# Decoder block on one core: x's rows at a pitch of 532 floats, a plain half-size message addition, and x's second layout loaded in one burst

## The chip, the core and the metric

The kernel runs on one core of one Trainium2 chip. The metric is the device time of one execution in microseconds (us). The kernel before took 665.99 us, the median of three runs (665.76 to 666.15). One more execution was recorded by the hardware profiler; every row shown here is from that one.

## What is computed

x has 32 batches of 64 channels by 512 positions, all float32. The reference is a decoder block of three layers, each added to its input and normalised over the 512 positions:

```python
q = jnp.transpose(x, (2, 0, 1))                       # 512 x 32 x 64
scores = jnp.einsum('lnc,lmc->lnm', q, q) / sqrt(64)  # for each position l: 32 x 32
prob = softmax(scores, axis=-1)
msg = jnp.einsum('lnm,lmc->lnc', prob, q)
x = _layernorm(x + (x + msg^T))                       # first layer, "x1"
x = _layernorm(x + xattn(x, ctx, Wq, Wk, Wv, Wo, bo, g))
x = _layernorm(x + ffn(x, w_gate, w_up, w_down))      # weights and activations quantised by groups of 32
```

The change is in the first layer. There the attention runs over the 32 batches, once for each of the 512 positions, so every operand of its small matrix products takes one float of each batch's row.

## The kernel before, in words

The five engines have their programs written out by hand, in a fixed order, and wait for each other on semaphores. SP (SyncE) issues all the transfers. The names and lines that matter:

- **x in SBUF.** `xt` holds x with two batches side by side on 128 partitions (64 channels each) and 16 rows of 512 floats along the partition, so from one batch's row to the next it is 2048 bytes. `xsw` behind it is the same with the two halves swapped; `both_x` and `x_by_batch` are views over both (L124 to L130). `load_x` (L375) brings x in four pieces; ScalarE (`swap_up`) and VectorE (`swap_down`, L1123) copy each piece across.
- **x's second layout.** `xq` (L131) has the batches on partitions: `load_xq` (L378) is called 32 times, 128 KB each. With three semaphores taken in turn, SP waits before transfer n until transfer n-3 has landed. Behind these on SP's queue stand `load_aw(1)`, `load_aw(2)`, `load_item(2)`, `load_aw(3)` and the first two context loads (L452 to L457).
- **The first layer.** The 512 positions go in 8 chunks of 16 positions from each quarter. `scores(c)` (TensorE, L2837) makes 64 products, each with a 64x32 stationary and a 64x32 moving operand read from `both_x` and `x_by_batch` with one float per 2048-byte row. `shift_scores` (VectorE, L1133 and L1134) takes the row maximum off, `exp_scores` (ScalarE, L1986) the exponential, `sum_scores` (VectorE, L1139 and L1140) the reciprocal sum, `norm_scores` (GpSimd, L631) scales, `transpose_probs` (VectorE, L1146) turns 32x32 blocks, and `spread_probs` (ScalarE, L1980) writes four masked copies with the mask `quarter` as scale. `messages(c, h)` (TensorE, L2865) multiplies them with `xq`, and `add_msg(c, h)` (VectorE, L1154) forms 2x + msg in `xt`. `scores(c)` from c = 2 on waits for `shift_scores(c-2)`.
- **TensorE's order**: scores(0), two weight transposes (L2792), scores(1) to scores(4), `project_wo` (L2798), scores(5), `project_b` (L2807), scores(6), scores(7), and then the messages, with transposes of the quantised weights and the first logits of the second layer between them. `messages(0, 0)` waits for all of `xq` (L2855).
- **VectorE's order** around it: shift(0), `scale_aw(0)` (a grouped maximum over 128x1376, L1087), `scale_item(0)`, sum(0), shift(1), clip_item(0), transpose(0), shift(2), sum(1), clip_aw(0), sum(2), transpose(1), shift(3), shift(4), sum(3), transpose(2), shift(5), and so on: the weights are quantised between the steps of the softmax.
- **The norm.** `x1_stats` and `x1_rsqrt` (L634) take mean and variance of a row and add `eps_tile` (1e-5).
- From about 112 us on the second layer (16 tiles of 128 rows) and then the FFN follow, with the same kind of hand-written order.

Of the kernel before, what the change touches and what calls it, by code (L numbers as in the profile page):

```python
# [8 lines left out]
ALU = mybir.AluOpType  # L9
# [9 lines left out]
P = 128  # L19
# [18 lines left out]
def decoder_kernel(nc, x, ctx_in, Wq, Wk, Wv, Wo, bo, g, w_gate, w_up, w_down, out):  # L38
    B, C, L = x.shape
    HID, DIM = Wq.shape  # L40
# [4 lines left out]
    T = B * C // P  # L45
    NJ = HID // P
    NT = L // P
# [9 lines left out]
    LG = L // 4  # L57
    CL = 16
    CQ = 8
    CHUNKS = LG // CL  # L60

    with ExitStack() as stack:
        def sb(name, shape, dt=F32):
            return stack.enter_context(nc.sbuf_tensor(name, shape, dt))

        def sem(name):
            return stack.enter_context(nc.semaphore(name))

        banks = stack.enter_context(nc.psum_tensor("banks", [P, 8, 512], F32))
        bank = [banks[:, i] for i in range(8)]  # L70
# [17 lines left out]
        shift = sb("shift", [P, 1])  # L88
        neg_mean = sb("neg_mean", [P, 1])
# [4 lines left out]
        square_o = sb("square_o", [P, 2])  # L94
        mv = sb("mv", [P, 2])
        eps_tile = sb("eps_tile", [P, 1])
        quarter = sb("quarter", [P, 4])
        vare = sb("vare", [P, 1])
        rstd = sb("rstd", [P, 1])
# [3 lines left out]
        mv1 = sb("mv1", [P, 2])  # L103
        vare1 = sb("vare1", [P, 1])
        rstd1 = sb("rstd1", [P, 1])
        mv2 = sb("mv2", [P, 2])
        vare2 = sb("vare2", [P, 1])
        rstd2 = sb("rstd2", [P, 1])
        neg_mean1 = sb("neg_mean1", [P, 1])
        shift1 = sb("shift1", [P, 1])  # L110
        neg_mean2 = sb("neg_mean2", [P, 1])
        shift2 = sb("shift2", [P, 1])

        AREA = 42400
        big = sb("big", [P, AREA])
        off = 0

        def cut(n):
            nonlocal off
            off += n  # L120
            assert off <= AREA
            return big[:, off - n:off]

        both_x = big[:, 0:2 * T * L].rearrange("p (n l) -> p n l", n=B)  # L124
        x_pairs = big[:, 0:2 * T * L].rearrange("p (s t l) -> p t s l", s=2, t=T)
        x_by_batch = (x_pairs[0:C], x_pairs[C:P, :, ::-1])

        xt = cut(T * L).rearrange("p (t l) -> p t l", t=T)

        xsw = cut(T * L).rearrange("p (t l) -> p t l", t=T)  # L130
        xq = cut(C * LG).rearrange("p (c l) -> p c l", c=C)  # L131

        off = T * L
        EK = cut(4 * NJ * L).rearrange("p (s b j n) -> p s b j n", s=2, b=2, j=NJ)
        EQ = cut(4 * NT * HID).rearrange("p (s b i h) -> p s b i h", s=2, b=2, i=NT)
        et_at = off
# [38 lines left out]
        off = sc_at  # L175
        sc = cut(3 * CL * B).rearrange("p (k l m) -> p k l m", k=3, l=CL)
        assert off <= sc_end
        off = et_at
        pT = cut(3 * CL * B).rearrange("p (k l m) -> p k l m", k=3, l=CL)
        assert off <= et_end  # L180
        off = pd_at
        pd = cut(2 * CL * P).rearrange("p (k l j m) -> p k l j m", k=2, l=CL, j=4)
        assert off <= aw_at
        off = aw_at
# [9 lines left out]
        won = wg_area[0:C, NJ * 7 * C:NJ * 7 * C + HID]  # L194
        woT = wg_area[:, NJ * 7 * C + HID:NJ * 8 * C + HID].rearrange("p (t c) -> p t c", t=NJ)

        off = T * L
        hs = cut(4 * FFN).rearrange("p (s n) -> p s n", s=4)
        h8 = cut(FFN // 4).bitcast(FP8)
        hk = [[cut(GH) for _ in range(3)] for _ in range(2)]  # L200
        spare = cut(L)
        assert off <= T * L + 4 * NJ * L

        off = T * L + 4 * NJ * L
        hq = cut(FT * P).bitcast(BF16).rearrange("p (s n) -> p s n", s=2)
        hqT = cut(FT * P).bitcast(BF16).rearrange("p (s f t) -> p s f t", s=2, f=FT)
        xo = cut(2 * L).rearrange("p (s n) -> p s n", s=2)
        assert off <= T * L + 4 * NJ * L + 2 * NT * HID
        yo = cut(2 * L).rearrange("p (s n) -> p s n", s=2)
        assert off <= T * L + 4 * (NJ * L + NT * HID)  # L210

        s = Semaphores()

# [17 lines left out]
        s.g8_ready = sem("g8_ready")  # L231

        s.x_loaded = [sem(f"x_loaded_{piece}") for piece in range(4)]
        s.xq_loaded = [sem(f"xq_loaded_{turn}") for turn in range(3)]
        s.swapped_up = sem("swapped_up")
        s.swapped_down = sem("swapped_down")
        s.scores_ready = sem("scores_ready")
# [135 lines left out]
        def _(sp):  # L373
# [3 lines left out]

            def load_xq(n):  # L378
                c, j = CQ * (n // 4), n % 4
                if n >= 3:  # L380
                    sp.wait_ge(s.xq_loaded[n % 3], 16 * (n // 3))
                sp.dma_start(xq[B * j:B * j + B, c:c + CQ], x[:, c:c + CQ, LG * j:LG * j + LG]).then_inc(s.xq_loaded[n % 3], 16)

            def load_aw(a):
                if a >= 3:
# [64 lines left out]
            for n in range(4 * C // CQ):  # L450
                load_xq(n)
# [120 lines left out]
        def _(pool):  # L572
            ch = Chain(pool, s.pool_chain)
            ch.link(pool.memset(ident[:], 0.0))
            ch.link(pool.affine_select(out=ident[:], in_=ident[:], compare_op=ALU.not_equal, fill=1.0, base=0,
                                       pattern=[[-1, P]], channel_multiplier=1))
            pool.tensor_copy(ident_bf[:], ident[:]).then_inc(s.consts, 1)
            pool.memset(eps_tile[:], 1e-5).then_inc(s.consts, 1)
            ch.link(pool.memset(quarter[:], 0.0))
            for j in range(4):  # L580
                ch.link(pool.memset(quarter[B * j:B * j + B, j:j + 1], 1.0))
            pool.memset(minus_half[:], -0.5).then_inc(s.consts, 1)
            ch.link(pool.memset(pair_ones[:], 0.0))
            for h in range(2):
# [46 lines left out]
                pool.tensor_tensor(p, p, s_sum[:, c % 3].unsqueeze(2).to_broadcast([P, CL, B]), ALU.mult  # L631
                                   ).then_inc(s.probs_ready, 1)

            def rsqrt(t, var, read, mv, vare, neg_mean, rstd, shift, done):  # L634

                pool.wait_ge(var, t + 1)
                if t:
                    pool.wait_ge(read, t)
                pool.tensor_tensor(neg_mean[:], zero[:], mv[:, 0:1], ALU.subtract)
                ch.link(pool.tensor_tensor(vare[:], mv[:, 1:2], eps_tile[:], ALU.add))  # L640
                ch.link(pool.tensor_tensor(rstd[:], vare[:], minus_half[:, 0:1], ALU.pow))
                pool.tensor_tensor(shift[:], neg_mean[:], rstd[:], ALU.mult).then_inc(done, 1)

            def x1_rsqrt(t):
                rsqrt(t, s.x1_var, s.x1_ready, mv1, vare1, neg_mean1, rstd1, shift1, s.x1_rstd)

            def x2_rsqrt(t):
                rsqrt(t, s.x2_var, s.x2_ready, mv2, vare2, neg_mean2, rstd2, shift2, s.x2_rstd)

            def fold_p(f, i):  # L650
                pool.wait_ge(s.q_exp_done, 4 * f + i + 1)
# [79 lines left out]
            shift_aw(4)  # L731
            shift_aw(5)
            x1_rsqrt(0)
            x1_rsqrt(1)
            dequant_aw(4)
            shift_aw(6)
            x1_rsqrt(2)
            fold_p(0, 0)
            dequant_aw(5)
# [343 lines left out]
        def _(dve):  # L1083
            ch = Chain(dve, s.dve_chain)
# [63 lines left out]

            def add_msg(c, h):
                dve.wait_ge(s.msg_ready, 2 * c + h + 1)  # L1150
                m = bank[(2, 6)[c % 2] + h].rearrange("p (l q) -> p q l", l=CL // 2)
                l0 = CL * c + CL // 2 * h
                r = xt.rearrange("p t (j l) -> p (t j) l", j=4)[:, :, l0:l0 + CL // 2]
                dve.scalar_tensor_tensor(out=r, in0=r, scalar=2.0, in1=m, op0=ALU.mult, op1=ALU.add  # L1154
                                         ).then_inc(s.msg_added, 1)

            def ln_stats(src, st, mv, done):
# [1626 lines left out]
        def _(pe):  # L2785
# [65 lines left out]
            def messages(c, h):  # L2851
                if h == 0:
                    pe.wait_ge(s.pd_ready, c + 1)
                if c == 0 and h == 0:
                    for turn in range(3):  # L2855
                        pe.wait_ge(s.xq_loaded[turn], 16 * len(range(turn, 4 * C // CQ, 3)))
                if c == 1 and h == 0:
                    pe.wait_ge(s.b_copied, 2)
                if c >= 2:
                    pe.wait_ge(s.msg_added, 2 * c + h - 3)  # L2860
                o = bank[(2, 6)[c % 2] + h]
                for l in range(CL // 2):
# [837 lines left out]
```

## Time and profile before

| | us |
|---|---|
| median of 3 runs | 665.99 |
| the profiled execution | 667.34 |
| its span in the trace | 665.5 |
| TensorE busy | 608.4 (91%) |
| VectorE busy | 559.1 (84%) |
| ScalarE busy | 486.0 (73%) |
| GpSimd busy | 481.9 (72%) |

The span is what the trace covers; the rest of the profiled time lies around it. TensorE is named PE in the rows, VectorE DVE, ScalarE ACT, GpSimd POOL. PEclk is TensorE's granted clock as a share of 2.4 GHz. A TensorE product of float32 operands appears as two records in the trace, so 64 products are 128 records.

### The profile page before, as it was taken

What the parts mean: (1) busy time and instruction counts of PE and PEld (TensorE: products, weight loads), DVE (VectorE), ACT (ScalarE), POOL (GpSimd) and SP (SyncE); (2) the same over time, 40 slices, a digit from 0 to 9 for tenths busy, and PEclk for the clock granted to TensorE, in tenths of its full rate; (3) what the DMA queues carried; (4) which work ended last, traced back from release to release, by engine and by line L of the source; (5) the groups of instructions that cost most, each with busy time, mean ns of one, the idle gap of its engine ahead of it and who ended that gap; (6) DMA issues with size and microseconds to landing.
All of it is one profiled execution on the core that took longest, in us unless ns stands there. A gap on an engine that the chain in (4) does not pass through costs nothing. (4 is left out here: it accounts for less than half of the span.)

```text
span 665.5 us, 13176 instructions
## 1 busy us (share of the span) xinstructions
PE 608.4 (91%) x4864; PEld 334.4 (50%) x4864; DVE 559.1 (84%) x801; ACT 486.0 (73%) x871; POOL 481.9 (72%) x634
## 2 busy tenths in 40 slices
PE   0757999889999999999999999999999979999993
PEld 0756997344444544455544455445444634444441
DVE  2779898799999999998998878888788369999992
ACT  5459664788899989888988879888888725443535
POOL 1165957679889989998888596786678544776673
PEclk9957999899999999999999999999999989999998
DMA  9547131000010011110101000000000003445645
GB/s 296 159 136 225 44 88 56 0 17 25 1 42 31 10 33 40 41 49 22 35 12 45 1 23 17 7 17 17 0 1 1 9 8 63 80 87 101 133 105 131
DMA packets 62912, 36.77 MB, mean 55 GB/s; under 512 B 45184, under 2 KB 53376, under 8 KB 62848
## 3 DMA queue, kind: packets, MB, share of 16 engines
q1 hardware_dynamic: 62848, 35.93, 21.5%
q8 instruction: 39, 0.64, 0.4%
q14 instruction: 25, 0.20, 0.1%
HBM read 21.82 MB, written 4.19 MB: 39 GB/s over the span
## 5 line engine op out<-in xcount | busy, mean ns | idle before, releaser
L1932 ACT ACTIVATE big<-banks 128x512 f32<-128x512 f32 x288 | 158.6, 601 | 22.0 <-PE banks L2923 8.9
L663 POOL TENSOR_TENSOR big<-big 128x512 f32<-128x512 f32 x128 | 132.3, 1061 | 21.2 <-DVE big L1187 21.0
L1164 DVE TENSOR_REDUCE big<-banks 128x1 f32<-128x512 f32 x128 | 83.1, 680 | 25.0 <-PE banks L2880 24.8
L1993 ACT ACTIVATE big<-banks,big 128x512 f32<-128x512 f32 x128 | 88.0, 695 | 19.3 <-DVE big L1164 18.1
L655 POOL TENSOR_TENSOR big<-big 128x512 f32<-128x512 f32 x64 | 82.2, 1289 | 10.1 <-ACT big L1998 10.0
L1170 DVE TENSOR_REDUCE big<-banks 128x16 f32<-128x1024 f32 x64 | 77.1, 1205 | 4.4 <-PE banks L2890 4.4
L1175 DVE TENSOR_TENSOR big<-banks,big 128x1024 f32<-128x1024 f32 x64 | 78.3, 1223 | 2.7 <-PE banks L2923 0.7
L2913 PEld LDWEIGHTS banks<-ident,big 128*128 128x128 f32 x512 | 56.6, 142 | 46.8 <-issue 22.3
L2923 PEld LDWEIGHTS banks<-ident,big 128*128 128x128 f32 x512 | 55.3, 141 | 46.6 <-issue 22.7
L2913 PE MATMUL banks<-ident,big 128*128 128x128 f32 x512 | 74.2, 281 | 2.6 <-ACT big L1993 1.5
L1998 ACT ACTIVATE big<-big 128x1024 f32<-128x1024 f32 x64 | 68.2, 1065 | 10.2 <-DVE big L1175 9.7
L2923 PE MATMUL banks<-ident,big 128*128 128x128 f32 x512 | 73.8, 280 | 1.5 <-ACT big L1932 1.2
L2880 PE MATMUL banks<-big,WkT 64*128 64x512 f32 x256 | 72.6, 644 | 0.1
L2890 PE MATMUL banks<-WqT,big 64*128 64x512 f32 x256 | 68.3, 610 | 3.4 <-ACT big L2027 2.4
L590 POOL TENSOR_SCALAR big<-big 128x16 f32<-128x16 f32 (+3 forms) x55 | 22.7, 412 | 63.4 <-DVE big L1088 38.0
L2937 PE MATMUL banks<-big 128*64 128x512 f32 x256 | 64.0, 606 | 0.4 <-issue 0.4
L2960 PE MATMUL banks<-big 128*64 128x512 f32 x256 | 60.6, 602 | 1.3 <-DVE big L1195 1.3
L2073 ACT ACTIVATE big<-banks 128x448 f32<-128x448 f32 (+1 forms) x48 | 26.1, 548 | 45.7 <-PE banks L2986 45.7
L2847 PE MATMUL banks<-big 64*32 64x32 f32 x1024 | 31.1, 314 | 27.8 <-ACT big L1932 16.5
L1092 DVE TENSOR_SCALAR big<-big 128x512 fp8e4<-128x512 f32 (+3 forms) x55 | 43.1, 785 | 12.3 <-POOL big L618 5.3
L2986 PE MATMUL banks<-wg_area,big 128*128 128x448 bf16 (+1 forms) x192 | 45.9, 362 | 4.3 <-DVE big L1235 4.3
L2986 PE MATMUL banks<-wuT,big 128*128 128x448 bf16 (+1 forms) x192 | 46.0, 363 | 0.0
(108 smaller groups left out, 1126.0 us busy)
## 6 DMA issues: line engine op xcount, KB each, us to landing
big<-in_x_dram SPq DMA_DIRECT2D x4, 1024.0 KB, 8.8
big<-in_x_dram SPq DMA_DIRECT2D x32, 128.0 KB, 2.8
big<-in_ctx_dram SPq DMA_DIRECT2D x16, 256.0 KB, 2.7
out_dram<-big SPq DMA_DIRECT2D x16, 256.0 KB, 2.4
big<-in_L_ffn_w_down_dram SPq DMA_DIRECT2D x4, 688.0 KB, 5.8
big<-in_L_ffn_w_gate_dram SPq DMA_DIRECT2D x10, 256.0 KB, 2.8
big<-in_L_ffn_w_up_dram SPq DMA_DIRECT2D x10, 256.0 KB, 3.0
big<-big SPq DMA_TRANSPOSE x48, 2.7
```

What stands on the lines that cost most here:

```text
L655: pool.tensor_tensor(qfold[:, i % 2], e[:, :, :, 0:DH // 2], e[:, :, :, DH // 2:DH], ALU.add).then_inc(s.q_folded, 1)
L663: pool.tensor_tensor(e, e, r, ALU.mult).then_inc(s.p_ready, 1)
L1164: dve.tensor_reduce(kneg[:, par, i:i + 1], bank[par], X, ALU.max, negate=True).then_inc(s.k_max_ready, 1)
L1170: ch.link(dve.tensor_reduce(qmax[:, i], q_pair, X, ALU.max))
L1175: dve.tensor_tensor(EQ[:, f % 2, :, i].rearrange("p b (h d) -> p b h d", d=DH), q_pair, qmax[:, i].unsqueeze(3).to_broadcast([P, 2, HEADS, ...
L1932: return act.activation(dst, src, ACT.Copy)
L1993: act.activation(EK[:, f % 2, par, i], bank[par], ACT.Exp, bias=kneg[:, par, i:i + 1], accum_out=ksum[:, f % 2, par, i:i + 1]).then_inc(s. ...
L2880: pe.matmul(bank[par][:], WkT[rows, P * i:P * i + P], ctxs[rows, f % 2], start=True, stop=True).then_inc(s.klog_ready, 1)
L2890: pe.matmul(bank[2 + par][:], xt[rows, f, P * i:P * i + P], WqT[rows, :], start=True, stop=True).then_inc(s.qlog_ready, 1)
L2913: last = pe.transpose(bank[4 + n % 2][:, P * j:P * j + P], EK[:, t % 2, par, j, P * i:P * i + P], ident[:])
L2923: last = pe.transpose(bank[4 + n % 2][:, P * i:P * i + P], EQ[:, t % 2, par, i, P * j:P * j + P], ident[:])
L2986: last = pe.matmul(o[:, 0:w], xqT[:, u % 2, f], wT[:, f, c0:c0 + w], start=(f == 0), stop=(f == KT - 1))
```

## The change

The rows of `xt` and `xsw` are laid 532 floats (2128 bytes) apart instead of 512; all areas behind them move up by 320 floats, and `pT`, which lay at the end of `xq` and at the start of `ET` at once, is anchored to the end of `xq`. The 32 transfers of `xq` all count on one semaphore and SP no longer waits between them; TensorE waits for that one. The mask holds 0.5 instead of 1.0, so the message comes out at half size, and the addition is x + msg/2 without the factor 2; as its result is half of 2x + msg, the norm adds a quarter of the epsilon, from a new one-column tile.

```diff
+        LP = L + 20
+        AREA = 42400 + T * (LP - L)
-        both_x = big[:, 0:2 * T * L].rearrange("p (n l) -> p n l", n=B)
-        x_pairs = big[:, 0:2 * T * L].rearrange("p (s t l) -> p t s l", s=2, t=T)
+        both_x = big[:, 0:2 * T * LP].rearrange("p (n l) -> p n l", n=B)
+        x_pairs = big[:, 0:2 * T * LP].rearrange("p (s t l) -> p t s l", s=2, t=T)
-        xt = cut(T * L).rearrange("p (t l) -> p t l", t=T)
-        xsw = cut(T * L).rearrange("p (t l) -> p t l", t=T)
+        xt = cut(T * LP).rearrange("p (t l) -> p t l", t=T)[:, :, 0:L]
+        xsw = cut(T * LP).rearrange("p (t l) -> p t l", t=T)[:, :, 0:L]
+        xq_end = off
-        off = et_at
+        off = xq_end
         pT = cut(3 * CL * B).rearrange("p (k l m) -> p k l m", k=3, l=CL)
...
-        s.xq_loaded = [sem(f"xq_loaded_{turn}") for turn in range(3)]
+        s.xq_loaded = sem("xq_loaded")
             def load_xq(n):
                 c, j = CQ * (n // 4), n % 4
-                if n >= 3:
-                    sp.wait_ge(s.xq_loaded[n % 3], 16 * (n // 3))
-                sp.dma_start(xq[B * j:B * j + B, c:c + CQ], ...).then_inc(s.xq_loaded[n % 3], 16)
+                sp.dma_start(xq[B * j:B * j + B, c:c + CQ], ...).then_inc(s.xq_loaded, 16)
...
+            pool.memset(eps_half[:], 0.25e-5)
-                ch.link(pool.memset(quarter[B * j:B * j + B, j:j + 1], 1.0))
+                ch.link(pool.memset(quarter[B * j:B * j + B, j:j + 1], 0.5))
-                ch.link(pool.tensor_tensor(vare[:], mv[:, 1:2], eps_tile[:], ALU.add))
+                ch.link(pool.tensor_tensor(vare[:], mv[:, 1:2], eps[:], ALU.add))
...
             def add_msg(c, h):
                 dve.wait_ge(s.msg_ready, 2 * c + h + 1)
-                m = bank[(2, 6)[c % 2] + h].rearrange("p (l q) -> p q l", l=CL // 2)
+                m = bank[(2, 6)[c % 2] + h].rearrange("p (l t j) -> p t j l", l=CL // 2, t=T)
                 l0 = CL * c + CL // 2 * h
-                r = xt.rearrange("p t (j l) -> p (t j) l", j=4)[:, :, l0:l0 + CL // 2]
-                dve.scalar_tensor_tensor(out=r, in0=r, scalar=2.0, in1=m, op0=ALU.mult, op1=ALU.add
-                                         ).then_inc(s.msg_added, 1)
+                r = xt.rearrange("p t (j l) -> p t j l", j=4)[:, :, :, l0:l0 + CL // 2]
+                dve.tensor_tensor(r, r, m, ALU.add).then_inc(s.msg_added, 1)
...
-                    for turn in range(3):
-                        pe.wait_ge(s.xq_loaded[turn], 16 * len(range(turn, 4 * C // CQ, 3)))
+                    pe.wait_ge(s.xq_loaded, 16 * 4 * C // CQ)
```

## Rows read from the trace of the kernel before

**Rows 1.** The page: TensorE's busy share, and the chain that ended last, by engine.

```profile
PE 608.4 (91%) x4864; PEld 334.4 (50%) x4864; DVE 559.1 (84%) x801; ACT 486.0 (73%) x871; POOL 481.9 (72%) x634
PE 7%; POOL 3%; DVE 2%; issue 1%; DMA 1%; ACT 1%; SPq 0%; POOLq 0%; DVEq 0%; ACTq 0%
```

**Rows 2.** Busy time by stretch: length, each engine's busy time, PEclk, DMA share, GB/s.

```profile
16.50:66.40 49.90, 34.79 (x1068) 33.45 (x1068) 40.04 (x36) 32.85 (x19) 21.60 (x14) 0.72 0.60 174
66.40:111.60 45.20, 45.20 (x553) 41.27 (x550) 40.26 (x59) 27.06 (x46) 33.84 (x32) 0.97 0.23 58
...
140.00:550.00 410.00, 400.85 (x2616) 201.12 (x2617) 355.86 (x524) 343.83 (x665) 330.15 (x423) 1.00 0.08 21
```

**Rows 3.** TensorE's timeline, 16 to 68 us: start, length, engine, line, operation, idle before.

```profile
16.51 3.95 PE L2847 MATMUL banks<-big 64*32 64x32 f32 x128 [16.51 <-ACT big L1932]
20.39 1.64 PE L2792 MATMUL banks<-ident,wg_area 128*128 128x128 f32 x8
21.95 7.55 PE L2847 MATMUL banks<-big 64*32 64x32 f32 x256
33.26 3.93 PE L2847 MATMUL banks<-big 64*32 64x32 f32 x128 [3.76 <-DVE big L1134]
...
55.66 1.61 PE L2807 MATMUL banks<-wg_area 64*64 64x64 f32 x32 [3.27 <-ACT wg_area L1932]
...
63.95 2.53 PE L2847 MATMUL banks<-big 64*32 64x32 f32 x78 [1.40 <-issue]
```

**Rows 4.** VectorE's timeline, 20 to 80 us.

```profile
21.83 8.18 DVE L1087 TENSOR_REDUCE big<-big 128x43 f32<-128x1376 f32 x1
...
32.52 0.69 DVE L1134 TENSOR_TENSOR big<-banks,big 128x512 f32<-128x512 f32 x1
...
49.10 3.42 DVE L1134 TENSOR_TENSOR big<-banks,big 128x512 f32<-128x512 f32 x1
...
52.55 0.69 DVE L1139 TENSOR_REDUCE big<-big 128x16 f32<-128x512 f32 x1
...
57.05 4.67 DVE L1146 STREAM_TRANSPOSE big<-big 128x512 f32<-128x512 f32 x1
60.13 3.33 DVE L1087 TENSOR_REDUCE big<-big 128x43 f32<-128x1376 f32 x1
...
66.59 0.72 DVE L1146 STREAM_TRANSPOSE big<-big 128x512 f32<-128x512 f32 x1
67.24 1.55 DVE L1087 TENSOR_REDUCE big<-big 128x43 f32<-128x1376 f32 x1
```

**Rows 5.** ScalarE's exponential: its first call, and one beside the messages.

```profile
21.95 7.30 ACT L1986 ACTIVATE big<-big 128x512 f32<-128x512 f32 x1 [5.49 <-DVE big L1134]
...
74.55 0.65 ACT L1986 ACTIVATE big<-big 128x512 f32<-128x512 f32 x1
```

**Rows 6.** Busy time by stretch, inside scores(1) and over scores(3); columns as in rows 2.

```profile
21.95:25.70 3.75, 3.75 (x134) 3.75 (x137) 3.75 (x1) 3.75 (x2) 0.00 (x0) 1.00 0.66 152
...
33.26:37.20 3.94, 3.93 (x128) 3.78 (x128) 0.00 (x0) 3.84 (x1) 3.69 (x4) 0.50 0.59 169
```

**Rows 7.** TensorE's timeline: three half chunks of messages.

```profile
74.32 7.49 PE L2865 MATMUL banks<-big 128*64 128x64 f32 x96
```

**Rows 8.** SP's timeline: the 32 transfers of xq, and the first one behind them.

```profile
19.04 34.76 SPq L382 DMA_DIRECT2D big<-in_x_dram  x32
53.84 0.93 SPq L388 DMA_DIRECT2D big<-in_L_ffn_w_down_dram  x2
```

**Rows 9.** Transfers while SP waits in turn, 24 to 54 us: queue's bytes and share, issues.

```profile
q1 hardware_dynamic: 7766, 3.74, 45.2%
...
big<-in_x_dram SPq DMA_DIRECT2D x29, 128.0 KB, 2.8
```

**Rows 10.** Busy time by stretch where the transfer engines are full; columns as in rows 2.

```profile
57.00:61.00 4.00, 4.00 (x142) 3.88 (x142) 4.00 (x3) 3.68 (x3) 3.79 (x1) 0.50 0.98 394
```

**Rows 11.** VectorE's message addition: calls, shortest, median and longest duration in ns.

```profile
L1154 DVE SCALAR_TENSOR_TENSOR big<-big,banks x16: 627/680/689, 72.4 to 110.7; 128x512 f32<-128x512 f32 x16
```

More of the change, by code:

```diff
@@ L96, in decoder_kernel @@
         eps_tile = sb("eps_tile", [P, 1])
+        eps_half = sb("eps_half", [P, 1])
         quarter = sb("quarter", [P, 4])
@@ L112, in decoder_kernel @@
         shift2 = sb("shift2", [P, 1])
-        AREA = 42400
+        LP = L + 20
+        AREA = 42400 + T * (LP - L)
         big = sb("big", [P, AREA])
@@ L122, in cut @@
             return big[:, off - n:off]
-        both_x = big[:, 0:2 * T * L].rearrange("p (n l) -> p n l", n=B)
-        x_pairs = big[:, 0:2 * T * L].rearrange("p (s t l) -> p t s l", s=2, t=T)
+        both_x = big[:, 0:2 * T * LP].rearrange("p (n l) -> p n l", n=B)
+        x_pairs = big[:, 0:2 * T * LP].rearrange("p (s t l) -> p t s l", s=2, t=T)
         x_by_batch = (x_pairs[0:C], x_pairs[C:P, :, ::-1])
-        xt = cut(T * L).rearrange("p (t l) -> p t l", t=T)
-        xsw = cut(T * L).rearrange("p (t l) -> p t l", t=T)
+        xt = cut(T * LP).rearrange("p (t l) -> p t l", t=T)[:, :, 0:L]
+        xsw = cut(T * LP).rearrange("p (t l) -> p t l", t=T)[:, :, 0:L]
         xq = cut(C * LG).rearrange("p (c l) -> p c l", c=C)
-        off = T * L
+        xq_end = off
+        off = T * LP
         EK = cut(4 * NJ * L).rearrange("p (s b j n) -> p s b j n", s=2, b=2, j=NJ)
@@ L195, in decoder_kernel @@
         woT = wg_area[:, NJ * 7 * C + HID:NJ * 8 * C + HID].rearrange("p (t c) -> p t c", t=NJ)
-        off = T * L
+        off = T * LP
         hs = cut(4 * FFN).rearrange("p (s n) -> p s n", s=4)
@@ L201, in decoder_kernel @@
         spare = cut(L)
-        assert off <= T * L + 4 * NJ * L
-        off = T * L + 4 * NJ * L
+        assert off <= T * LP + 4 * NJ * L
+        off = T * LP + 4 * NJ * L
         hq = cut(FT * P).bitcast(BF16).rearrange("p (s n) -> p s n", s=2)
@@ L207, in decoder_kernel @@
         xo = cut(2 * L).rearrange("p (s n) -> p s n", s=2)
-        assert off <= T * L + 4 * NJ * L + 2 * NT * HID
+        assert off <= T * LP + 4 * NJ * L + 2 * NT * HID
         yo = cut(2 * L).rearrange("p (s n) -> p s n", s=2)
-        assert off <= T * L + 4 * (NJ * L + NT * HID)
+        assert off <= T * LP + 4 * (NJ * L + NT * HID)
         s = Semaphores()
@@ L379, in load_xq @@
                 c, j = CQ * (n // 4), n % 4
-                if n >= 3:
-                    sp.wait_ge(s.xq_loaded[n % 3], 16 * (n // 3))
-                sp.dma_start(xq[B * j:B * j + B, c:c + CQ], x[:, c:c + CQ, LG * j:LG * j + LG]).then_inc(s.xq_loaded[n % 3], 16)
+                sp.dma_start(xq[B * j:B * j + B, c:c + CQ], x[:, c:c + CQ, LG * j:LG * j + LG]).then_inc(s.xq_loaded, 16)
             def load_aw(a):
@@ L632, in norm_scores, with rsqrt @@
                                    ).then_inc(s.probs_ready, 1)
-            def rsqrt(t, var, read, mv, vare, neg_mean, rstd, shift, done):
+            def rsqrt(t, var, read, mv, eps, vare, neg_mean, rstd, shift, done):
                 pool.wait_ge(var, t + 1)
@@ L644, in x1_rsqrt @@
             def x1_rsqrt(t):
-                rsqrt(t, s.x1_var, s.x1_ready, mv1, vare1, neg_mean1, rstd1, shift1, s.x1_rstd)
+                rsqrt(t, s.x1_var, s.x1_ready, mv1, eps_half, vare1, neg_mean1, rstd1, shift1, s.x1_rstd)
             def x2_rsqrt(t):
-                rsqrt(t, s.x2_var, s.x2_ready, mv2, vare2, neg_mean2, rstd2, shift2, s.x2_rstd)
+                rsqrt(t, s.x2_var, s.x2_ready, mv2, eps_tile, vare2, neg_mean2, rstd2, shift2, s.x2_rstd)
             def fold_p(f, i):
```

## The prediction, made before the change was run

> **What bounds the kernel now.** I read the page first. TensorE is busy 91% of the span, more than any other engine; the chain that ended last accounts for only about a sixth of the span, its end, and so says nothing of the first layer, where the change is [rows 1]. Next I cut the span by stage [rows 2]. From 66.4 us to 111.6 us TensorE is busy all the time, and in the long middle, 140 to 550 us, 98% of it (400.85 of 410.00). Whatever reaches 66.4 us earlier should therefore reach the end earlier by about as much: the orders are fixed, and what follows is held by TensorE's own work. The stage in front is different. From 16.5 to 66.4 us TensorE works 34.79 of 49.90 us, so it stands idle 15.1 us, and its clock was granted at full speed only part of the time (0.72 on average).
>
> TensorE's timeline says what it waits for there [rows 3]. Chunks of scores take 3.9 us each (3.95 and 3.93 for one, 7.55 for two) and between them lie gaps of 3 to 4 us that end with VectorE's subtraction (L1134) or a ScalarE copy. Yet VectorE has little to do. Its timeline shows why it is late [rows 4]: the grouped maximum takes 8.18 us at 21.83 and 1.55 us at 67.24; the block transpose 4.67 us at 57.05 and 0.72 us at 66.59; the subtraction 3.42 us at 49.10 and 0.69 us at 32.52. ScalarE's exponential takes 7.30 us at 21.95 and 0.65 us at 74.55 [rows 5]. Every long one lies over a chunk of scores and ends with it: the exponential from 21.95 to 29.25 over the two chunks from 21.95 to 29.50 [rows 3, 5]. The short ones run with no scores beside them; the last of them run beside the messages, which keep TensorE just as busy, with operands that don't step by 2048 bytes [rows 4, 5, 7]. 
>
> **The pitch of 532 floats.** It removes no instruction. The rows then start at 2128 bytes times n, and 32 of them fall on many different offsets modulo 2048 or 512. If the stalls go, VectorE's four longest rows give back 8.18 - 1.55, 4.67 - 0.72, 3.42 - 0.69 and 3.33 - 1.55, together 15.1 us [rows 4]. Its 40.04 us of busy time before 66.4 us [rows 2] then hold at most 25 us of work, to be done in some 35 us. ScalarE and GpSimd gain likewise. What is late next? I walked the written order with the short durations. After scores(0) at 20.5 us, shift(0) (two passes of 0.69 us), scale_aw(0) (1.55 and a short one, 1.8), scale_item(0) (0.9) and sum(0) (0.69 and a reciprocal, 0.95) end at 25.6 us [rows 4], when scores(1) is just done; shift(1) is ready at 27.3 and scores(3) wants it at 29.5. GpSimd's two weight scalings and norm_scores(0), 6.2 us by an estimate from its undisturbed calls beside the messages, let transpose(0) end at about 30.7, so shift(2) is ready at 32.1, wanted at 33.4. shift(3) is ready at 36.9, wanted at 38.1, after project_wo; shift(4) and shift(5) have 4 us to spare. ScalarE's copies for the two small projections are in time too (41.1 us, wanted at 41.9). So all gaps close, the narrowest by 1.2 us.
>
> Then TensorE goes through this stage in its own work: 34.79 us from 16.5, which ends at 51.3 instead of 66.4. **Term: -15.1 us.** I take the scores' own 3.9 us as unchanged, for this reason: in scores(3), at a granted clock of 0.50 (1.2 GHz), 128 records take 3.93 us, one in 30.7 ns; in scores(1) and (2), the first of them at 1.00 (2.4 GHz), 256 take 7.55 us, one in 29.5 ns [rows 3, 6]. So the clock is hardly what limits them; and the messages, without that pitch, need 7.49 us for 96 records, 78 ns for twice the columns [rows 7], which is no faster per column (1.2 ns against 0.96). Reading with steps is slow there too. Bounds: no gain, or at most half of a chunk.
>
> **The burst.** Now SP takes 34.76 us for 32 transfers and gets to the next load at 53.84 [rows 8]. While it does, 3.74 MB move in 30 us at 45.2% of the engines' time [rows 9]; at full share the same would take 13.6 us, and all 4.2 MB about 15. SP is behind the first weight loads until about 23.5 us, so xq is in at about 39 us in the best case, at 53.8 + 2.8 = 56.6 in the worst (no faster than now) [rows 8, 9]. Nearer the best, since only three were ever under way: I take 42. The messages want it at 51.3. Without the burst, the last of xq would hold them until 56.6; so the two parts need each other, and the burst is worth 5.3 of the 15.1 us. Its own cost: TensorE reads its instructions by transfers on the same engines. The one gap that nothing shown releases ("issue", 1.40 us, at 62.6 [rows 3]) is just behind a stretch in which the transfer engines are 0.98 busy [rows 10]. The burst makes a stretch like that of some 15 us, over four chunks. Bounds: nothing, or 1.4 us for each of four, 5.6. I take one: **+1.5 us**. Behind the burst on SP's queue the loads of the weights come 12 us or so earlier than now; scale_aw(1), which VectorE reaches at about 45 us instead of 60.13 [rows 4], needs one issued by 39, and that is as close as it gets: a late one costs up to 2 us there, hidden by 4 us of slack on TensorE. The first context load is wanted 15 us earlier and issued as much earlier.
>
> **The addition.** Sixteen additions of 0.68 us [rows 11] become plain ones; the nearest row is the subtraction with an operand from the same memory, 0.69 us [rows 4]. 0 to 0.2 us in all, on VectorE, beside messages that take 2.5 us for each: **0**. One memset more stands in GpSimd's first microseconds, when it has nothing else to do: 0. The half-size mask and epsilon change values only.
>
> **x's load and swap.** x comes in 2048-byte rows either way; only where they land moves, off the even boundaries. The first scores start at 16.51 us, released by the last swap of the last piece [rows 3]; if each row cost a little more this start would slip, 0 to 1 us. I take 0. The swaps read padded rows: VectorE's might lose its double rate, ScalarE's is longer and sets the start.
>
> **Sum.** -15.1 + 1.5 = -13.6 us. Against the profiled execution, 667.34 (a span of 665.5 and 1.8 around it), that is 653.7; this one stood 1.35 above the median of the runs, 665.99, so the median I forecast is **652.4 us**.
>
> **The rivals.**
> *The scores get faster too.* For it: all others starve while they run, as if TensorE used up what it can get from that part of memory, and the duration hardly heeds the clock [rows 5, 6]. Against it: the messages. If a chunk took 3.1 us, the eight would give 6 us more, but VectorE's chain then decides (shift(5) can't end before about 39 us, and two chunks follow), and so does xq at 42. Worth 3 to 7 us more: 645 to 649, at most 642. The Trainium skill (TensorE: Matmul & The Clock Gate, section "Wait — 56ns, not 53.3ns?") says that matmuls never start less than about 25 ns apart, however few their columns. By that, an estimate from that page, the 30.7 ns could fall by a fifth and no more. Chance 0.22.
> *The burst or the load is slow.* xq comes in at 56.6 as now, or several instruction reads are late: 656 to 664.6. Chance 0.14.
> *The pitch does nothing.* The change would not do what it says: the long instructions are long for another reason, say the transfers of xq beside them. Against it: they go back to 0.7 us in the gaps between chunks, where the same transfers run on (VectorE's 0.69 us at 32.52 [rows 4]). Then TensorE's gaps stay, xq was in before 66.4 anyway, and the time is 666, within 0.2%. The Trainium skill (SBUF — State Buffer, section "SBUF: two separate sides") says this too: TensorE, ScalarE and VectorE's own port never wait on anyone. The trace disagrees, by 7.30 us against 0.65 for one and the same exponential. Chance 0.05.
> *Slower: instruction reads starve in the burst.* TensorE needs a new block of instructions about once a chunk. With 32 transfers queued, its reads stand behind them on every engine. Each chunk after the first would then stall; from 2.2 us for each of seven (15.1 / 7) the gain is gone, and at 3 us the time is 666.0 - 15.1 + 21 = 672. For it: the 1.40 us gap. Against: the burst is short (15 us, so four chunks, not seven), and TensorE went from scores(0) to scores(1) and (2) without a gap (16.51 to 29.50 us, with the first weight loads under way) [rows 3]. Chance 0.06.
>
> **The numbers.** The forecast's case (649 to 656) has 0.53. A measurement of this kernel tells about 0.2%, 1.3 us, from no change. Faster by more than that: 0.53 + 0.22 + 0.14 = 0.89; within it 0.05; slower 0.06. The range takes in the forecast, most of the case with faster scores and the near part of the slow burst: 644 to 658.
>
> **What would show it.** In the changed kernel's trace no exponential (L1986 before) over 0.9 us and no grouped maximum over 2 us during scores; messages that start at 51 to 53 us; scores at 3.9 us a chunk; SP through its 32 transfers by 40 us; the stages from there on of the same length as now, 45 us for the messages. I am wrong if long instructions stay during scores, if TensorE waits at the messages for a transfer, if gaps named "issue" fill the chunks, or if a head start of some 14 us at the messages is not there at the end.

## The result, and the profile after

The changed kernel takes 656.12 us in the median of its four runs (651.63 to 658.01), beside 665.88 for the kernel before. The ratio is 0.9835, with a 95% interval of 0.9804 to 0.9867: 1.3 to 2.0% faster, 9.8 us by the medians and about 11 by the ratio. Six further runs of the same kernel, beside the last experiments, gave a median of 654.50 and the ratio 0.984 (0.9813 to 0.9867). The forecast was 652.4, range 644 to 658. The changed kernel scatters over 6 us; the kernel before over 1 us here and over 3 to 6 beside the experiments, where it was run more often.

The page of the changed kernel, profiled at 655.72 us, and busy time by stretch (columns as in [rows 2]). The first stretch ends where the messages now begin, the second is as long as it was before:

```profile
PE 597.9 (91%) x4864; PEld 322.6 (49%) x4864; DVE 542.0 (83%) x801; ACT 463.5 (71%) x871; POOL 472.2 (72%) x635
```

```profile
16.50:52.60 36.10, 22.39 (x1068) 20.61 (x1068) 24.31 (x38) 11.10 (x19) 14.64 (x16) 0.70 0.92 238
...
52.60:97.80 45.20, 45.20 (x555) 41.49 (x550) 38.30 (x56) 26.30 (x44) 30.49 (x31) 0.98 0.28 55
```

The first stage went from 49.9 to 36.1 us. The same 1068 records keep TensorE busy for 22.39 us instead of 34.79, VectorE for 24.31 instead of 40.04, ScalarE for 11.10 instead of 32.85 [rows 2]. TensorE has no gap in the second stretch. The stage of the messages ends with the start of TensorE's L2901, before the change and after:

```profile
111.60 0.66 PE L2901 MATMUL banks<-ident,big 128*128 128x128 f32 x4
```

```profile
98.34 0.66 PE L2901 MATMUL banks<-ident,big 128*128 128x128 f32 x4
```

So it runs from 52.63 to 98.34 us, 45.7 us, where it ran from 66.41 to 111.60, 45.2.

ScalarE's and VectorE's timelines, answering to [rows 4, 5]:

```profile
20.13 0.63 ACT L1987 ACTIVATE big<-big 128x512 f32<-128x512 f32 x1 [3.81 <-DVE big L1136]
...
29.36 0.63 ACT L1987 ACTIVATE big<-big 128x512 f32<-128x512 f32 x1 [8.11 <-DVE big L1136]
```

```profile
24.54 1.59 DVE L1089 TENSOR_REDUCE big<-big 128x43 f32<-128x1376 f32 x1 [4.44 <-DMA big<-in_L_ffn_w_down_dram]
...
47.36 1.59 DVE L1089 TENSOR_REDUCE big<-big 128x43 f32<-128x1376 f32 x1 [2.18 <-DMA big<-in_L_ffn_w_down_dram]
...
51.03 1.55 DVE L1089 TENSOR_REDUCE big<-big 128x43 f32<-128x1376 f32 x1
```

Nothing is held up any more. The exponential at 29.36 lies over the scores from 29.38 and takes 0.63 us, not 7.30; the first one, at 20.13, has no scores beside it. The grouped maximum at 51.03 lies over the scores from 51.22 and takes 1.55, not 8.18; those at 24.54 and 47.36 lie mostly in TensorE's gaps. But ahead of these two there are now waits for weight loads. TensorE's timeline, answering to [rows 3]:

```profile
16.37 2.25 PE L2848 MATMUL banks<-big 64*32 64x32 f32 x128 [16.37 <-ACT big L1933]
19.09 1.76 PE L2793 MATMUL banks<-ident,wg_area 128*128 128x128 f32 x8 [0.47 <-DMA g<-in_L_xattn_g_dram]
20.79 3.74 PE L2848 MATMUL banks<-big 64*32 64x32 f32 x214
27.36 0.91 PE L2848 MATMUL banks<-big 64*32 64x32 f32 x42 [2.84 <-issue]
29.38 1.61 PE L2848 MATMUL banks<-big 64*32 64x32 f32 x86 [1.10 <-DVE big L1136]
32.19 0.91 PE L2848 MATMUL banks<-big 64*32 64x32 f32 x42 [1.20 <-issue]
34.82 2.57 PE L2848 MATMUL banks<-big 64*32 64x32 f32 x128 [1.73 <-DVE big L1136]
...
39.38 2.23 PE L2848 MATMUL banks<-big 64*32 64x32 f32 x128 [1.37 <-DVE big L1136]
...
51.22 1.48 PE L2848 MATMUL banks<-big 64*32 64x32 f32 x78 [3.44 <-issue]
52.63 7.78 PE L2865 MATMUL banks<-big 128*64 128x64 f32 x96
```

A chunk of scores takes 2.25 us instead of 3.95. The gaps shrank but did not go. Most of what is left is named "issue": TensorE has nothing to wait for that the profile shows and still does nothing, in the middle of a chunk. The sums by releaser, up to the messages, and SP's timeline around the burst, answering to [rows 8]:

```profile
PE banks L2848 <- issue: 7.5, 3, 3.4
...
PE banks L2848 <- DVE big L1136: 4.2, 3, 1.7
...
PE banks L2808 <- ACT wg_area L1933: 1.5, 1, 1.5
```

```profile
18.89 23.15 SPq L383 DMA_DIRECT2D big<-in_x_dram  x32
42.07 2.10 SPq L389 DMA_DIRECT2D big<-in_L_ffn_w_down_dram  x2
```

SP has issued all of xq at 42.04 instead of 53.8. The last transfer lands 4.0 us after its issue, so xq is in at about 46, and it is no longer what the messages wait for.

**What the gaps named issue are.** The page counts the packets of the instruction queue:

```profile
q8 instruction: 39, 0.64, 0.4%
```

**Behind the messages.** The head start is 13.8 us where the messages begin (52.63 against 66.4) and 11.6 at the end of the span. Where it shrinks is seen by one line that runs twice a tile, TensorE's L2967, here one of its first calls and its last, before and after:

```profile
165.89 1.02 PE L2967 MATMUL banks<-big,pair_ones 128*128 128x512 f32 x2
...
558.76 1.08 PE L2967 MATMUL banks<-big,pair_ones 128*128 128x512 f32 x2
```

```profile
154.05 1.02 PE L2967 MATMUL banks<-big,pair_ones 128*128 128x512 f32 x2
...
547.16 1.08 PE L2967 MATMUL banks<-big,pair_ones 128*128 128x512 f32 x2
```

It is 11.84 us at the first of these and 11.60 at the last, so the long middle passes a head start on almost whole, and the loss lies before 154 us. Half a microsecond of it went in the stage of the messages (13.26 us at L2901). Behind that the granted clock differs. Of the kernel before, and of the changed one:

```profile
119.50:121.00 1.50, 1.46 (x6) 0.69 (x7) 0.93 (x3) 1.50 (x4) 1.25 (x3) 0.84 0.00 0
121.00:124.00 3.00, 3.00 (x12) 1.69 (x10) 0.98 (x1) 2.92 (x7) 2.67 (x6) 0.51 0.00 0
124.00:128.00 4.00, 4.00 (x26) 1.52 (x25) 3.20 (x5) 3.08 (x7) 2.11 (x3) 1.00 0.00 0
```

```profile
106.30:107.80 1.50, 1.50 (x4) 0.49 (x4) 0.63 (x2) 1.50 (x4) 1.26 (x3) 0.50 0.00 0
107.80:111.00 3.20, 3.20 (x12) 2.08 (x12) 1.23 (x1) 2.40 (x7) 2.92 (x5) 0.50 0.00 0
111.00:115.00 4.00, 4.00 (x23) 1.34 (x19) 2.63 (x4) 2.52 (x6) 1.60 (x1) 0.79 0.00 0
```

In both, TensorE idles at the start of the second layer, where the messages have ended and the norm of the first rows is awaited, and some of its work behind that runs at 1.2 GHz. Worked out from the mean clocks of these rows, that is about 3.4 us of work in the kernel before (from about 120.5 us on) and about 6.4 us in the changed one (from its start at 106.3 us). Three more microseconds at half speed cost 1.5 by this estimate, and the head start shrinks by 1.4 there (13.25 us at 119.54 against 106.29, then 11.84). In the repeat of the same kernel (experiment 10) the last call of L2967 starts at 546.66, 12.1 us ahead, from messages that began only 12.4 us ahead: there almost nothing was lost. So this part of the loss varies from run to run.

### The profile page after: what moved, and what is told of

Same layout as the page of the kernel before. It is cut to its first block and busy times, and to the rows that moved or that the text cites. A ratio compares the mean times of both kernels' runs of the same rounds, so it can differ in the third digit from the quotient of the medians.

```text
span 653.9 us, 13176 instructions
## 1 busy us (share of the span) xinstructions
PE 597.9 (91%) x4864; PEld 322.6 (49%) x4864; DVE 542.0 (83%) x801; ACT 463.5 (71%) x871; POOL 472.2 (72%) x635
## 5 line engine op out<-in xcount | busy, mean ns | idle before, releaser
L3003 PE MATMUL banks<-wdT,big 128*128 128x512 bf16 (+1 forms) x176 | 41.1, 379 | 5.0 <-DVE sum_o L1273 3.0
```

## The experiments

Each diff is against the changed kernel. Times are medians; the ratio is to the kernel before on the same chip.

**1. The pitch without the burst.** SP's wait in turn is put back; the plain addition stays.

```diff
-        s.xq_loaded = sem("xq_loaded")
+        s.xq_loaded = [sem(f"xq_loaded_{turn}") for turn in range(3)]
 def load_xq(n):
+    if n >= 3:
+        sp.wait_ge(s.xq_loaded[n % 3], 16 * (n // 3))
```

> The changed kernel with SP's wait in turn (three transfers of xq under way) put back; pitch 532 and the plain addition stay. Theory (the burst's price is late instruction reads and late weight loads): scores keep 2.2 to 2.6 us a chunk, the gaps named issue inside the scores fall from 7.5 us to under 1.5, the grouped maximum of scale_aw(0) starts by 22 us instead of 24.5, TensorE is through scores(7) by 46 us, and then the messages wait for xq until 55 to 57, so the time is 657 to 661, above the changed kernel. Rival (TensorE outruns its instruction reads by itself, since a chunk now takes 2.3 us): issue gaps of over 4 us stay in the scores without the burst. Second rival (the pitch is worth all of it and xq was never late): messages start by 48 us and the time is under 653.

It took 661.88 us, ratio 0.9927 (0.9910 to 0.9944). TensorE's timeline from scores(7) on:

```profile
48.07 1.48 PE L2850 MATMUL banks<-big 64*32 64x32 f32 x78 [1.43 <-issue]
58.78 7.43 PE L2868 MATMUL banks<-big 128*64 128x64 f32 x96 [9.23 <-DMA big<-in_x_dram]
```

TensorE is through scores(7) at 49.55 us, 3 us ahead of the changed kernel, and then waits 9.23 us for xq. So the two parts do need each other, and xq in turns became the bound, as both the forecast and this expectation had it, though later than expected (58.78 us, and 661.88 for the whole). The issue gaps fell from 7.5 to 4.8 us, not to under 1.5. The first rival's sign, over 4 us of them without the burst, is there; experiment 5 takes up whether they are TensorE's own.

**2. The burst alone**, with the plain addition, at the old pitch.

```diff
-        LP = L + 20
+        LP = L + 0
```

> The changed kernel with the pitch back at 512 floats; the burst and the plain addition stay. Theory (the stalls come from the pitch alone): exponentials of 3 to 7 us and a grouped maximum of over 5 us beside scores are back, a chunk of scores takes 3.8 to 4.0 us, xq is in at 42 us and is of no use, the messages start at 64 to 69 us, time 664 to 670. Rival (transfers of xq beside them made the instructions long, and the early end of these is what helped): long instructions end with the transfers at 42 us, messages start by 58, time 655 to 660.

It took 666.30 us, ratio 0.9986 (0.9969 to 1.0003): nothing. ScalarE's and TensorE's timelines:

```profile
22.06 4.52 ACT L1987 ACTIVATE big<-big 128x512 f32<-128x512 f32 x1 [5.57 <-DVE big L1136]
...
48.10 3.92 ACT L1987 ACTIVATE big<-big 128x512 f32<-128x512 f32 x1 [3.10 <-DVE big L1136]
```

```profile
56.49 7.60 PE L2848 MATMUL banks<-big 64*32 64x32 f32 x256
64.03 7.39 PE L2865 MATMUL banks<-big 128*64 128x64 f32 x96
```

The last exponential of 3.9 us lies at 48.1 us, over scores(5), 8 us after SP had issued the last of xq (39.9). Transfers of xq don't make it long, the scores at a pitch of 2048 bytes do. Two chunks take 7.60 us again. This run also holds the plain addition: it costs nothing that can be measured. Its 16 calls have a median of 0.675 us here and 0.691 in the changed kernel, against 0.680 [rows 11]. One thing is not separated: with the pitch, all areas behind `xt` and `xsw` move as well. The scores read only these two, so their own gain is the pitch's; that the neighbours are freed by it too, and not by the places of their own data, is argued from their ending with the scores.

**3. Six under way.** As experiment 1 with six semaphores in turn.

```diff
+        s.xq_loaded = [sem(f"xq_loaded_{turn}") for turn in range(6)]
+    if n >= 6:
+        sp.wait_ge(s.xq_loaded[n % 6], 16 * (n // 6))
```

> The changed kernel with SP waiting in turns of six transfers of xq instead of not at all. Theory (only the depth of the queue makes other reads late): xq is in by 40 to 44 us, because six under way move about as much as 32, while the issue gaps in the scores fall from 7.5 us to 2 to 4 and scale_aw(0) starts by 23 us; messages start at 47 to 50.5 us, time 650 to 654. Rival (the transfer engines' full share makes them late, not the depth): gaps and late loads as in the changed kernel, messages at 52 to 53, time 655 to 657.

It took 655.74 us, ratio 0.9834 (0.9817 to 0.9851), the same as the changed kernel. In the profiled run SP was through with xq at 46.2 us, the gaps in the scores came to 5.4 us and the messages began at 50.16, with an issue gap of 1.17 us inside them. Six in flight gain nothing by the median: fewer gaps, but VectorE waits until 51.16 us for the weight load behind xq. The theory's start of the messages (50.16) and its fewer gaps came true, though 5.4 us is more than its 2 to 4; xq, through SP only at 46.2, and the time, 655.74 against 650 to 654, did not.

**4. Another pitch.** 2112 bytes, 33 times 64.

```diff
-        LP = L + 20
+        LP = L + 16
```

> The changed kernel with rows 528 floats apart (2112 bytes, 33 times 64) instead of 532 (2128 bytes, 133 times 16). Theory 1 (any pitch that isn't a power of two spreads the rows enough): scores 2.2 to 2.6 us a chunk, exponentials 0.6 to 0.9 us, time as the changed kernel, 654 to 658. Theory 2 (only a pitch of an odd number of 16-byte lines spreads them; at 2112 bytes all 32 reads keep the same 16 bytes of each 64): scores 2.6 to 3.5 us a chunk and exponentials over 1 us beside them, time 657 to 663.

It took 655.39 us, ratio 0.9813 (0.9788 to 0.9838), with exponentials of 0.63 to 0.65 us beside scores and scores at 2.44 to 2.56 us a chunk against 2.25:

```profile
16.37 2.44 PE L2848 MATMUL banks<-big 64*32 64x32 f32 x128 [16.37 <-ACT big L1933]
```

```profile
28.50 0.65 ACT L1987 ACTIVATE big<-big 128x512 f32<-128x512 f32 x1 [7.03 <-DVE big L1136]
```

Theory 1 holds at this pitch: it needs no odd multiple of 16 bytes. Only these two pitches off 2048 bytes were run. The chosen one is 0.2 us a chunk better, which nothing shows in the time.

**5. No xq beside the scores.** SP waits for scores(7) before the first of the 32.

```diff
+            sp.wait_ge(s.scores_ready, CHUNKS)
             for n in range(4 * C // CQ):
                 load_xq(n)
```

> The changed kernel with SP waiting for scores(7) before it issues the 32 transfers of xq, so that no transfer of xq or of what is queued behind it runs beside scores(1) to scores(7). The messages then come late and the time, 672 to 685, says nothing; the gaps named issue do. Theory (traffic makes the instruction reads late): under 0.5 us of issue gaps in the scores, from 7.5 with the burst and 4.8 with three under way. Rival (a chunk of 2.3 us is shorter than TensorE's instruction reads take on idle engines): 1 to 2 us at each of three places remain, 3 to 5 us in all.

One execution, 675.83 us, in which the messages start at 72.28, since xq comes late. Who TensorE waited for in the scores:

```profile
PE banks L2849 <- DVE big L1137: 5.9, 3, 2.8
PE banks L2849 <- issue: 2.2, 3, 1.4
```

The gaps named issue come to 2.2 us without transfers of xq, 4.8 with three under way, 7.5 (and 9.2 in the repeat) with all of them. Most of it is traffic, as far as one or two executions of each can say. 2.2 us lies between the theory's bound and the rival's. In its two larger gaps, 1.45 us up to 26.17 and 0.60 in scores(7), the transfer engines' share is 0.00; the tail of the first weight loads lies ahead of the first, up to 24.5 us. So a small rest, the 0.60 us at least, is TensorE's own pace: it uses up a block of instructions sooner than the next one is there.

**6. The messages' operand off its power of two.** xq's rows at 528 bytes, x's at 2112 to make room.

```diff
-        LP = L + 20
+        LP = L + 16
-        xq = cut(C * LG).rearrange("p (c l) -> p c l", c=C)
+        xq = cut(C * (LG + 4)).rearrange("p (c l) -> p c l", c=C)[:, :, 0:LG]
```

> The changed kernel with xq's 64 rows laid 132 floats (528 bytes) apart instead of 128 (512 bytes), and x's rows 528 apart to make room. The messages' stationary operand steps by that pitch. Theory (any step by a high power of two slows TensorE's own reading, as the scores went from 3.93 to 2.25 us a chunk): three half chunks of messages take 4.5 to 6.5 us instead of 7.5, the stage of the messages (52.6 to 97.3 us in the changed kernel) gets 4 to 12 us shorter, time 644 to 652. Rival (512 bytes are no trouble, since nothing starves beside the messages; their 78 ns are the cost of 64 columns read in steps and of their moving operand): 7.4 to 7.5 us as before, time 654 to 657.

It took 653.38 us, ratio 0.9826 (0.9798 to 0.9854), not told apart from the changed kernel by these runs. TensorE's timeline in the messages:

```profile
60.49 6.02 PE L2865 MATMUL banks<-big 128*64 128x64 f32 x96
...
89.33 4.07 PE L2865 MATMUL banks<-big 128*64 128x64 f32 x64 [2.46 <-ACT big L1981]
```

Three half chunks take 6.02 us instead of 7.5 [rows 7]: a step of 512 bytes cost a fifth, though it starved nobody. It is xq's step and not x's, since experiment 4 has x's rows at 2112 bytes too and 7.42 us here. But the messages as a whole, to their last product, gained 3.2 us (51.85 to 93.40, against 52.63 to 97.35), less than the 4 to 12 expected: there is an issue gap of 1.25 us in them, and near their end TensorE waits 2.46 us for ScalarE's spread_probs. The theory holds for the operand, and not for the time.

**7. The loads behind the burst, one by one.**

```diff
             load_aw(1)
+            sp.wait_ge(s.aw_loaded[1], 16)
             load_aw(2)
+            sp.wait_ge(s.aw_loaded[2], 16)
             load_item(2)
             load_aw(3)
+            sp.wait_ge(s.aw_loaded[0], 32)
             load_ctx(0)
```

> The changed kernel with SP waiting for each of the three weight loads behind the burst before it issues the next, so that they and the context loads don't fill the engines at 46 to 52 us. Theory (the 3.44 us issue gap at 47.8 us is TensorE's instruction read behind these loads): the gap falls under 2 us and the messages start at 50 to 51.5 us instead of 52.6, time 1 to 2.5 us under the changed kernel. Rival (something else sets that gap): 3 us or more of it stay, no change.

It took 651.85 us, ratio 0.9796 (0.9772 to 0.9820), from 650.58 to 654.01. The busy time of the stretch of the large gap in the changed kernel, then of the stretch with the gap at the same place here, and TensorE's timeline behind that:

```profile
48.00:52.00 4.00, 0.79 (x50) 0.78 (x52) 3.93 (x6) 0.78 (x2) 2.58 (x3) 0.91 1.01 387
```

```profile
46.00:48.60 2.60, 1.55 (x97) 1.43 (x88) 1.29 (x1) 2.58 (x4) 0.00 (x0) 0.84 0.33 68
```

```profile
48.69 1.46 PE L2851 MATMUL banks<-big 64*32 64x32 f32 x78 [1.14 <-issue]
50.09 7.40 PE L2868 MATMUL banks<-big 128*64 128x64 f32 x96
```

With the transfer engines at a share of 0.33 instead of 1.01, the gap is 1.14 us instead of 3.44, and the messages begin 2.5 us earlier. The theory's signs came true. The time is lower by 2.7 to 4.3 us than the two medians of the changed kernel, but the intervals of the ratios overlap (0.9804 to 0.9867 there), so by the times alone the gain is not shown.

**8. The second subtraction ahead of the weight work.**

```diff
             shift_scores(0)
+            shift_scores(1)
             scale_aw(0)
             scale_item(0)
             sum_scores(0)
-            shift_scores(1)
```

> The changed kernel with VectorE's shift_scores(1) moved ahead of scale_aw(0), which waits for a weight load until 24.5 us. Theory (that late load costs TensorE the 1.10 us gap ahead of scores(3) and nothing else, since the later gaps follow from GpSimd's and VectorE's chain and from instruction reads): that gap is gone, messages start 0 to 1 us earlier, time within 1.5 us of the changed kernel. Rival (the late load delays the whole chain): messages start by 50 us, time under 654.

It took 657.34 us, ratio 0.9876 (0.9841 to 0.9910), in runs from 654.88 to 659.92, so it gains nothing; the profiled one is the slowest of these. There the gap ahead of scores(3) from VectorE is gone, but the issue gaps are 16.3 us and the messages begin at 56.84:

```profile
PE banks L2848 <- issue: 16.3, 6, 3.5
PE banks L2848 <- DVE big L1136: 0.9, 1, 0.9
```

Neither theory nor rival has the messages later by 4.2 us: the wait removed came back as another one. The next experiment follows it up.

**9. The same with three under way** (the edits of 8 and 1 together).

> The kernel with shift_scores(1) first, whose issue gaps in the scores came to 16.3 us beside the burst, with only three transfers of xq under way. Theory (the gaps are instruction reads held up by the burst, and with VectorE out of the way they are all that TensorE waits for): the gaps fall to 4 to 8 us, TensorE is through scores(7) by 47 us, the messages then wait for xq until 56 to 59 us. Rival (a quicker order of work alone makes TensorE outrun its reads): 12 us or more of gaps stay.

One execution, 660.37 us:

```profile
PE banks L2868 <- DMA big<-in_x_dram: 5.1, 1, 5.1
PE banks L2850 <- issue: 4.8, 3, 1.9
```

16.3 us of issue gaps beside the burst and 4.8 without it, from the same order of work: the burst makes the difference. TensorE was through scores(7) at 50.5 us, later than the theory's 47, for it waits 5.1 us for VectorE again. Each of the two is one execution only.

**10. The changed kernel once more.**

> The changed kernel once more, unaltered, on the same chip as the next ones. Its runs so far lie between 651.6 and 658.0. Expected: median 654 to 657.5, messages starting at 50 to 55 us, the later the more issue gap there is in the scores.

Median 654.50, from 652.66 to 659.00. In its profile (span 652.3) the gaps in the scores come to 9.2 us, one of them 4.62 us in scores(7), and the messages begin at 54.00, 1.4 us later than in the first profile.

**11. What helped, together** (edits 6 and 7).

> Both edits that helped, together: the three weight loads behind the burst one by one, and xq's rows at 132 floats with x's at 528. Theory (they remove different things, an instruction read's delay ahead of the messages and part of the messages' own 7.5 us): messages start at 50 to 51 us, three half chunks take 6.0 us, time 2 to 4 us under either alone is out of reach since ScalarE's spread_probs then decides in the messages; 648 to 651. Rival (ScalarE and VectorE already decide the stage of the messages): no better than the one-by-one loads alone, 651 to 653.

It took 649.78 us (646.87 to 652.15), ratio 0.9766 (0.9747 to 0.9785), beside 654.50 for the changed kernel on the same chip. The two intervals don't touch, so this is faster than both kernels.

```profile
51.95 6.03 PE L2868 MATMUL banks<-big 128*64 128x64 f32 x96
...
80.08 2.19 PE L2868 MATMUL banks<-big 128*64 128x64 f32 x32 [0.84 <-ACT big L1984]
```

The messages begin at 51.95 here, after 8.1 us of issue gaps, which this kernel still has. One of them is in scores(7), nearly as long as in the changed kernel:

```profile
50.41 1.61 PE L2851 MATMUL banks<-big 64*32 64x32 f32 x78 [2.68 <-issue]
```

The transfer engines' share in this gap is only 0.15 (47.7 to 50.4 us). But it was 0.87 ahead of it, under the first of the spaced loads, and the instruction packet starts at 48.0 us, when that is over. So in this execution the spaced loads did not bring the messages to 50 to 51 us, and the gain lies in the messages. Whether the two edits together beat the spaced loads alone (0.9772 to 0.9820) is not settled; the intervals touch.

## Why the prediction was right, point by point

**The pitch ends the stalls: right.** No instruction is long beside the scores, and they are long again with everything else changed and only the pitch put back (experiment 2). The Trainium skill (SBUF — State Buffer, section "SBUF: two separate sides") has ScalarE and TensorE never wait on each other; an exponential of 7.30 us at one pitch and 0.63 at another contradicts that. What inside the memory the rows share is not shown; only that 2048 bytes is bad for the neighbours, 2112 and 2128 are not, and that 512 (the messages) slows TensorE and, as far as seen, nobody else.

**"I take the scores' own 3.9 us as unchanged": wrong.** This is the step that failed. A chunk takes 2.25 us. The pitch held TensorE as it held its neighbours, and its work in the stage fell by 12.4 us (34.79 to 22.39). I had two facts for that, the starving of all others and a duration that hardly heeded the clock, and set them aside for the messages, which are no quicker per column. But the messages stepped by a power of two themselves: off it they gain a fifth (experiment 6), so they were no clean yardstick. The rule of the Trainium skill that I set beside it (TensorE: Matmul & The Clock Gate, section "Wait — 56ns, not 53.3ns?": matmuls start at least about 25 ns apart) I had applied to records. The records now start 17.6 ns apart (128 in 2.25 us), so applied like that the trace disagrees. Counted by float32 products, of two records each, it is 35 ns, and 61 before, above the rule's figure. No run here shows which of the two the figure counts.

**"All gaps close": wrong.** With TensorE 12 us quicker, VectorE's chain decides: 4.2 us of waits for the subtraction, 1.5 for a ScalarE copy and 0.5 for a small load are left, where the walk had 0. The walk's own times were fair: it had shift(1) at 27.3 us, shift(2) at 32.1, shift(3) at 36.9; they ended at 29.3, 34.8 and 39.3. Two microseconds of that are the weight load, which VectorE awaited until 24.54 us instead of finding it there at 21.9.

**The burst, +1.5 us: far too small.** The issue gaps are 7.5 us in one profile and 9.2 in the other, at most 2.2 of them TensorE's own (experiment 5). I had counted one late instruction read of 1.4 us, and bounded it by four. They are up to 4.6 us long. The largest is not in the burst: it lies behind the weight and context loads that follow at once on SP's queue (experiment 7), whose earlier start I had booked at no cost to TensorE. The burst itself is longer than the 15 us I gave it: SP takes 23.15 us to issue it, and xq came in at about 46 us, not 42, still well before the messages.

**The sum.** 34.8 us of work and 1.5 of gaps were forecast from 16.5 us to the messages, so 52.8; there are 22.4 of work and 13.7 of gaps, 52.6. The start of the messages is right by luck: two errors of 12 us cancel. The rival "the scores get faster too" came true in its mechanism, and the late instruction reads of two other rivals took back what it would have given. Of my own signs, the short exponentials and the start of the messages came true; the 3.9 us a chunk and SP's 40 us (42.04) did not, and the gaps named issue, which I had listed as a sign of being wrong, are there.

**From the messages on: nearly right.** Their stage took 45.7 us instead of 45.2, and from 154 us on the head start held but for 0.2. In the first profile 1.4 us went in between, where the granted clock stood at 1.2 GHz for longer, and next to nothing in the repeat; no term was there for it.

**The other rivals.** "The pitch does nothing" is refuted by experiments 1 and 2. "Instruction reads starve" happened, at about half its deciding price. "The burst or the load is slow" came true by its second half: x's load and the start of the scores are where they were (16.37 against 16.51 us) and xq held nobody, but several instruction reads were late. The measured 656.12 us stands at the near end of that rival's 656 to 664.6 and just outside my own case, 649 to 656.

## What to carry to other kernels

When instructions of several engines take five times their usual length and end together with another engine's, look at the step with which that engine reads; a row pitch off a high power of two may free the neighbours and the reader too. And a reader set free outruns what feeds it: look for what becomes late next among the things that no semaphore names, the instruction reads above all, before queueing transfers as deep as they will go. Behind a burst, a pause between large loads may let such a read through; it did in experiment 7 and hardly in experiment 11.

## What the runs showed that I had not expected

- A step of 512 bytes in the stationary operand costs TensorE time (7.5 against 6.02 us for three half chunks) though no neighbour was seen to be held up by it.
- Issue gaps in the scores by traffic: 2.2 us with no xq, 4.8 with three transfers under way, 7.5 and 9.2 with all.
- scale_aw(0)'s load of 688 KB lands 4.0 us after its issue in both kernels with the old pitch, with the burst behind it or without (experiment 2), and after 5.9 to 7.4 us at 2112 or 2128 bytes; 6.1 even where no xq follows (experiment 5). Something other than the burst of xq makes it slower when the scores run faster; in experiment 5 an instruction packet starts at 18.8 us beside it, where the kernel before has its first after 16 us at 21.8. Whether that has to do with it is not shown. This was not followed up and stays open.
- How the changed kernel comes to scatter over 6 us was seen only in single profiles: the sum of its issue gaps (7.5 and 9.2 us) and the length of a half-clock stretch near 108 us both differ between them. Which weighs more is open.
